# VectorE masks a dense tile inside a burst of top-k operations

## The reference, cut to what matters

```
def _pk(x, Wq_pk, pk_keys):
    q = (x @ Wq_pk).reshape(b, n, P, HEADS, DIM_KEY).transpose(2, 0, 1, 3, 4)
    sim = jnp.einsum('pbnhd,pkhd->pbnhk', q, pk_keys)
    scores, idx = jax.lax.top_k(sim, PK_TOPK)
    index = (idx0[..., :, None] + idx1[..., None, :]).reshape(b, n, HEADS, PK_TOPK * PK_TOPK)
    score = (scores[0][..., :, None] + scores[1][..., None, :]).reshape(...)
    final_scores, pk_idx = jax.lax.top_k(score, FINAL_TOPK)
    ...
k = jnp.einsum('bnhk,bnhkd->bnhd', kv_scores, keys_table[ind])
v = jnp.einsum('bnhk,bnhkd->bnhd', kv_scores, values_table[ind])
```

## Time and profile before

| what | value |
|---|---|
| median of the timed runs | 3286.44 us |
| lowest and highest | 3283.16, 3289.22 us |
| span of the profiled execution | 3919.1 us |
| TensorE busy in it | 2986.0 us (76%) |
| VectorE busy in it | 2791.8 us (71%) |
| ScalarE busy in it | 2037.7 us (52%) |
| GpSimd busy in it | 2052.1 us (52%) |
| mean granted clock of TensorE | 0.869 of full speed |

### The profile page before, as it was taken

One profiled execution on the slowest core, in us unless ns is written; L12 is line 12 of the kernel. 1 busy time (PEld: TensorE's weight loads), 2 busy tenths in 40 slices (PEclk: granted clock), 3 DMA queues, 4 the chain that ended last, 5 costly groups with the idle time before them and its releaser, 6 DMA issues. The chain is left out here.

```text
span 3919.1 us, 39389 instructions
## 1 busy us (share of the span) xinstructions
PE 2986.0 (76%) x9782; PEld 1393.2 (36%) x9782; DVE 2791.8 (71%) x9999; ACT 2037.7 (52%) x4498; POOL 2052.1 (52%) x2095
## 2 busy tenths in 40 slices
PE   4861667868786768878787878787878878787888
PEld 2430222424333323334333433333333433333443
DVE  7678777777777777777768786767768887864423
ACT  3231544555555655556555655555555755555522
POOL 3011666566666666565656655555656565655300
PEclk7985777989788989999889989888988989998999
DMA  1001121212121212111111111121211111111000
GB/s 37 22 8 52 45 66 43 59 46 58 48 58 48 58 48 59 45 53 51 54 50 48 56 45 55 41 57 44 58 45 52 53 51 48 47 56 42 23 3 3
DMA packets 85626, 179.86 MB, mean 46 GB/s; under 512 B 40177, under 2 KB 41107, under 8 KB 85398
## 3 DMA queue, kind: packets, MB, share of 16 engines
q0 software_dynamic: 66560, 135.40, 13.2%
q1 hardware_dynamic: 18838, 41.94, 3.4%
HBM read 176.15 MB, written 1.05 MB: 45 GB/s over the span
## 5 line engine op out<-in xcount | busy, mean ns | idle before, releaser
L1356 POOL DMA_INDIRECT mx_G<-in_kv_table,mx_slot_i x2048 | 1998.7, 976 | 1388.0 <-issue 605.7
L1384 PE MATMUL mx_acc<-mx_W,mx_table 128*128 128x512 f32 x2048 | 1179.6, 660 | 3.4 <-ACT mx_kvT L1586 3.2
L1743 DVE SCALAR_TENSOR_TENSOR mx_W<-mx_D,mx_W 128x512 f32<-128x512 f32 x1024 | 698.5, 682 | 352.7 <-ACT mx_W L1579 257.9
L1579 ACT ACTIVATE mx_W<-mx_D 128x512 f32<-128x512 f32 x1024 | 607.5, 594 | 525.0 <-remote 235.1
L1647 ACT ACTIVATE mx_GT<-mx_G,mx_slot_w 128x128 f32<-128x128 f32 x2048 | 759.1, 495 | 3.9 <-DVE mx_KVs L1960 1.9
L1374 PE MATMUL mx_D<-mx_U,mx_pick_b 96*128 96x512 bf16 x1024 | 434.3, 424 | 117.6 <-remote 53.8
L1384 PEld LDWEIGHTS mx_acc<-mx_W,mx_table 128*128 128x128 f32 x2048 | 437.4, 215 | 214.9 <-issue 130.4
L1603 ACT ACTIVATE mx_PT<-mx_area 128x512 f32<-128x512 f32 x480 | 246.7, 516 | 455.1 <-remote 145.2
L1396 PE MATMUL mx_O<-mx_PT,mx_KVs 128*65 128x512 f32 (+3 forms) x768 | 333.2, 517 | 130.7 <-ACT mx_OT L1595 86.7
L1410 PE MATMUL mx_area<-mx_KTa,mx_QTa 64*128 64x512 f32 (+3 forms) x384 | 202.9, 613 | 248.0 <-DVE mx_mx_part L1978 83.0
L1960 DVE TENSOR_REDUCE mx_KVs<-mx_GT 128x128 f32<-128x2048 f32 x128 | 292.0, 2281 | 7.5 <-ACT mx_GT L1647 7.3
(11 more groups left out here) (382 smaller groups left out, 4439.9 us busy)
## 6 DMA issues: line engine op xcount, KB each, us to landing
mx_table<-in_kv_dense SPq DMA_DIRECT2D x64, 512.0 KB
mx_G<-in_kv_table,mx_slot_i POOLq DMA_INDIRECT x2048
tz_table<-in_c_dft SPq DMA_DIRECT2D x1, 2048.0 KB
tz_table<-in_c_idft SPq DMA_DIRECT2D x8, 256.0 KB, 2.6
out_h<-mx_xc SPq DMA_DIRECT2D x4, 256.0 KB
mx_G<-in_c_pick SPq DMA_DIRECT2D x1, 528.0 KB
st_h<-in_tok_W,em_ids POOLq DMA_INDIRECT x32
st_keys<-in_pk_keys SPq DMA_DIRECT2D x1, 512.0 KB, 3.8
```

Of the source, the lines that this page charges most:

```text
L1356: pool.indirect_dma_start(G[g % RING][:, r, :], None, a["kv_table"], bass.IndirectOffsetOnAxis(slot_i[n % 2][:, k, r:r + 1], 0))\
L1384: pe.matmul(acc[:, :], table[:, tile, :], W[c % TILE_RING][:, :], start=(tile == 0), stop=(tile == TILES - 1)).then_inc(applied, 1)
L1579: act.activation(W[c % TILE_RING][:, :], D_ps[c % 3][:, :], ACT.Exp).then_inc(p_done, 1)
L1743: dve.scalar_tensor_tensor(W[c % TILE_RING][:, :], D_ps[c % 3][:, :], 0.0, W[c % TILE_RING][:, :], ALU.is_ge, ALU.mult).then_inc(w_done, 1)
```

## The change

In 17 of the 32 positions of the chain, the steps that are bursts now call `other_work()` too, some way into the burst: after four of eight maxima, after two of the three or four items of an index and replace step, after two of four pairs of indices in steps 9 and 10, before the third of five pairs of sums, after four of eight in steps 14, 17 and 18. The mask of the position is then done there, and not at the position's end. For 15 slots with both a top-k chain and dense tiles that is 34 masks a slot, 510 of 1024. No instruction, wait or DMA is added or taken away.

```diff
                 if k in (0, 1):
                     dve.wait_ge(x_taken, cnt.x["sim", n, 2 * tau + k] + 1)
                     for j in range(8 * k, 8 * k + 8):
+                        if j % 8 == 4:
+                            other_work()
                         done["first", k] = chain.mark(dve.max(seat(V, j, lo8), S[:, j // 4, j % 4, :]))
                 if 2 <= k < 7:
                     chain.wait(done["first", 0 if k < 4 else 1])
                     for j in range(16 * (k - 2) // 5, 16 * (k - 1) // 5):
+                        if j == 16 * (k - 2) // 5 + 2:
+                            other_work()
                         if j % 2:
...
                 if k in (7, 8):
                     chain.wait(done["struck", k - 7])
                     for j in range(8 * k - 56, 8 * k - 48):
+                        if j % 8 == 4:
+                            other_work()
...
                 if k in (9, 10):
                     chain.wait(done["second", k - 9])
                     for j in range(8 * k - 71, 8 * k - 64, 2):
+                        if j % 8 == 5:
+                            other_work()
...
                     for a0, na, nb in RECTS:
+                        if a0 == 2:
+                            other_work()
...
                 if k == 14:
                     chain.wait(done["sums"])
                     for u in range(2 * GROUP):
+                        if u == GROUP:
+                            other_work()
...
                 if k in (15, 16):
                     chain.wait(done["best", k - 15])
                     for u in range(GROUP * (k - 15), GROUP * (k - 14)):
+                        if u % GROUP == 2:
+                            other_work()
...
                 if k == 17:
                     for u in range(2 * GROUP):
+                        if u == GROUP:
+                            other_work()
...
                 if k == 18:
                     for u in range(2 * GROUP):
+                        if u == GROUP:
+                            other_work()
```

## The result

The changed kernel takes 3304.14 us (median of four, 3301.08 to 3305.12) against 3286.32 beside it (3283.16 to 3289.22): a ratio of 1.0044 on record, 95% interval 1.0032 to 1.0056. The quotient of the two medians is a little larger (1.0054, 17.8 us), with four runs on each side. A second set gave 1.0041 (1.0028 to 1.0055), and there the medians are 13.8 us apart. So the kernel is slower by some 14 us, where the forecast was +6: the sign and the main place were right, the size was not.

The account below looks back on a forecast made before the run. No engine fills the span: VectorE has more work over p = 17 to 39, TensorE over p = 40 to 63. Terms +6.0 (`add_heads`), +3 (burst waits) and -3 (masks) gave +6 us, from 3286.4 to about 3293 us, range 3283 to 3305.

Parts of the forecast that it names:

- The bound: Whole span: no engine fills it; VectorE has more work over p = 17 to 39, TensorE over p = 40 to 63.
- Rows 6: Profile rows of slot 15 at p = 5, read as layer-1 attention score products covering `add_heads`, with the chain through them.
- `add_heads` at p = 5: Slots 3 to 15: the mask passes `add_heads`, so TensorE's transposes start 0.60 us later; +6.0 us, bounds 3.6 to 7.8.
- Other things passed: `add_heads` at p = 11, 20 and 49, `combine`, layernorm, gathers and table loads: no cost, taken as 0, bounds 0 to 2.4 us.
- The wait inside the burst: VectorE stands at a late exponential with half a burst behind the mask; +3 us, bounds 0 to 8.3.
- turn from ahead to behind: Near p = 15 to 21 and 35 to 39, where VectorE stops being ahead of the exponential; there a burst wait costs 0.55 us.
- Masks that TensorE waits for: Nine of 80 waits are in changed positions and get shorter by part of a burst; -3 us, ends nothing and 7 us.
- Own criteria: Profile after: waits for `add_heads` and exponential grow, scores' waits for masks shrink, TensorE's wait for maxima changes by at most some 10 us.
- The faster rival: Earlier masks pay more: half a us saved in each of 15 slots, `add_heads` hidden, about 3279 us; chance 0.22.
- The rival of burst waits: VectorE turns from ahead to behind three times a slot, 0.5 us each in 15 slots: 22.5 us lost, 3309 us; chance 0.12.

Follow-up runs that it names:

- the second profile: The unchanged kernel profiled again, as the first profile was 632.7 us longer than its timed runs; it took 3287.9 us, with a profiled span of 3286.0.
- p = 5 alone: The kernel before with only the mask of p = 5 (step 2 of tau 0, 15 masks) moved into the divided burst, ahead of `add_heads`: 3297.1 us, ratio 1.0028.
- p = 17 to 39 alone: The kernel before with only the 165 masks of p = 17 to 22 and 35 to 39 moved into their bursts: 3292.2 us, ratio 1.0013.
- the two parts that hold these masks: Two kernels against before: only the 330 masks outside p = 5 and p = 17 to 39 moved, ratio 1.0019; only those of p = 17 to 39, 1.0013.
- without p = 5: The changed kernel with the 15 masks of p = 5 put back behind `add_heads`: 3295.4 us, ratio 1.0021 to before.
- `add_heads` first: `add_heads` put ahead of the step. At p = 5: before 0.9990, changed kernel 1.0005. At every position: before 0.9994, changed kernel 1.0002.
- divided or not: Undivided: the kernel before with the mask of p = 5 between the whole step 2 and `add_heads`, 3296.1 us, ratio 1.0027; divided: 3297.1 us, 1.0028.

## Why the prediction came out as it did

**The bound.** That the first profile was the same work with more idle time in it, and that this idle time would be gone in a timed run, held for the larger part: the second profile's span is 3286.0. That busy times would be the same did not hold, since the clock was lower in the first. And one reading took cover for slack. Rows 6 were read as layer-1 products hiding `add_heads` in slot 15. In the second profile they do, but with nothing to spare: TensorE comes to the transposes of slots 7, 11 and 15 just as `add_heads` ends, without idle time before and with 0.65 to 0.66 us after, and these stretches are 0.73 to 0.74 us longer. Only in slots 8 and 12, where p = 5 to 7 is 6.48 us before and after, are the transposes covered.

**`add_heads` at p = 5: +6.0 predicted.** Place, order and releaser were right, and the wait grew by 8.8 us (weight loads; 7.2 for products) for "some 6". The term was mis-sized: in time it is 9.2 us alone, or 7.6 taken out of the whole. The step that failed is the price of a late transpose, taken as the mask's 0.60 us and nothing else. Two things were missing. The mask also waits for its exponential with `add_heads` behind it (0.14 us in slot 7). In slots 10 and 14 this is more, since the mask of p = 4 stands in its burst too, and four maxima that were ahead of it now follow its wait. Slot 14, before:

```profile
2574.27 0.69 DVE L1743 SCALAR_TENSOR_TENSOR mx_W<-mx_D,mx_W 128x512 f32<-128x512 f32 x1 [0.80 <-ACT mx_W L1579]
...
2578.43 0.65 PE L1489 MATMUL mx_X<-mx_ident_b,mx_PC 128*96 128x128 bf16 x8 [2.15 <-DVE st_h L2007]
...
2579.13 1.02 PE L1384 MATMUL mx_acc<-mx_W,mx_table 128*128 128x512 f32 x2
```

and after:

```profile
2587.74 0.69 DVE L1743 SCALAR_TENSOR_TENSOR mx_W<-mx_D,mx_W 128x512 f32<-128x512 f32 x1 [1.30 <-ACT mx_W L1579]
...
2588.34 0.59 DVE L1759 MAX8 mx_V<-mx_S 128x8 f32<-128x64 f32 x4
...
2592.97 1.09 PE L1489 MATMUL mx_X<-mx_ident_b,mx_PC 128*96 128x128 bf16 x8 [3.22 <-DVE st_h L2025]
...
2594.28 1.92 PE L1384 MATMUL mx_acc<-mx_W,mx_table 128*128 128x512 f32 x2
```

The idle time is 3.22 - 2.15 = 1.07 us longer, and that is 0.50 from p = 4 and the rest from p = 5. Then the second thing: after the longer wait TensorE runs the same two products in 1.92 us for 1.02. The stretch is 11.58 - 7.62 = 4.0 us longer from a wait that grew by 1.07. Over the 13 slots the busy time is 4.9 us longer, and the stretches are 12.1 us longer in the trace (6.4 in that of p = 5 alone, whose time says 9.2). Not all of the 12.1 is the mask of p = 5, as slots 9, 10 and 14 show.

**Other things passed: 0 predicted (0 to 2.4).** At p = 11 TensorE does wait longer, by 0.6 us in slots 8 and 12. "TensorE has a position of its own work in between" was wrong there: the transposes of line 1498 come 0.05 us after `add_heads`. There are two such slots, 8 and 12, and not four: `add_heads` runs at p = 11 in slots 16 and 20 too, but without a step of the chain. The size is within the bounds.

**The wait inside the burst: +3 predicted (0 to 8.3).** The size of p = 17 to 39 alone, 4.3 us, is near it; the mechanism as told isn't shown. From slot 7 on no mask waits at p = 17 to 22, inside a burst or at its end, so no turn from ahead to behind costs half a burst there. That a wait inside a burst comes off later idle time, as the prediction said, is seen behind p = 48: VectorE's idle time ahead of masks, in slots 1 to 15, grows from 51.1 to 60.0 us over p = 49 to 54 and falls from 20.0 to 10.1 over p = 55 to 63. Where a wait inside a burst could be shown to cost, it was at p = 4 of slots 10 and 14, which the prediction didn't have.

**Masks that TensorE waits for: -3 predicted.** The mechanism was right and its price was not. TensorE's idle time at these waits fell by some 5 us in slots 2 to 15 (7.6 to 2.7), more than the 3 that the prediction took; 0.38 us of it in slot 3, for the 0.39 that it named for such a burst. But the two parts that hold these masks are slower by 6.2 and 4.3 us. What failed is the step from a wait to time: the prediction took each shortened wait off the sum. The runs show no gain in time, and where these 5 us are lost again stays open. The whole-span row (118.3 to 121.5) hides this, because it also has the waits for masks that didn't move, and waits put down to a mask that had ended well before. By the rule that the prediction quoted from the Trainium skill (Perfetto Trace Analysis, section Optimizing Scalar/DVE Operations), breaking up work on an engine that isn't saturated can let it complete sooner. The traces bear that out for the masks (1.80 to 1.42 us of wait in slot 3) and not for the kernel, which became slower.

**Own criteria.** The wait for `add_heads` grew, as asked, and so did VectorE's for the exponential (243.3 to 264.8). The row of scores that wait for masks didn't fall. TensorE's wait with weight loads for maxima (1978) went from 187.1 + 71.8 to 189.5 + 85.2, +15.8 us, more than the 10 that the prediction allowed. With p = 5 alone, where nothing at p = 17 to 39 moved, it is 193.3 + 88.1: so it isn't the order within that stretch. The reading behind the criterion stands: over p = 17 to 39 of slots 2 to 15 VectorE is busy for 838.9 of 855.7 us before and 841.2 of 862.5 after, 98%. The wait is a poor test of it, because it also tells how fast TensorE was: in this stretch TensorE is busy for 688.7 us and waits for maxima for 247.3 before, and 678.8 and 269.8 with p = 5 alone. Over all traces but the first the two go against each other (a correlation of -0.8). What makes the stretch itself 6.8 us longer stays open.

**The sum.** +6 + 3 - 3 became about +9, +4 and +6 by the parts' own times, which overlap, since the whole is some 14. That 3304 lies inside the forecast's bounds (3283 to 3305) is in part luck: the positions that were to give 3 us back cost 6. The faster rival had its shorter waits and not its time. The rival of burst waits named nearly this time (3309), but not for this reason: with `add_heads` ahead the bursts are divided as before, and the change costs 2 to 5 us over the same order and no longer 14. What stays open is the cost of the other positions: 0.2% without p = 5, but only 0.08 to 0.15% with `add_heads` first (1.0002 and 1.0005 over 0.9994 and 0.9990), and no single place in the traces carries it.

## What to carry to other kernels

Before an operation is put earlier in an in-order list, look at what it passes and who waits for that: the 15 masks of p = 5, of 510 moved, made half of the loss or more, because 13 of them pass `add_heads`, and 11 of these delay products for which TensorE has nothing else to do. A wait that gets shorter is not yet time: some 5 us of waits for masks went away here and the kernel got no faster by it. Price a longer wait of TensorE not by its length alone, but by the granted clock of the products behind it as well. And profile the kernel before a second time when its profiled span is far from its timed one: what seems hidden may be hidden by idle time only.

## What the runs showed of the hardware

TensorE's clock has two levels here, 2.4 and 1.2 GHz (granted 1.00 and 0.50), and it fell behind waits that were little longer. In slot 14 it was at 1.00 over the whole stretch with an idle time of 2.15 us; after 3.22 us idle two products took 1.92 us for 1.02, and a score product 0.63 for 0.38. The score products of p = 6 that took 0.63 us are 3 of 13 before, 7 and 8 in the two traces of the change, 6 with p = 5 alone, divided or not, and 1 to 5 in the others. The length of the wait doesn't settle it alone: in slots 3 to 5 of before the clock fell after 2.76 to 2.81 us, in slot 6 not after 2.81; with p = 5 alone it fell in slot 9 after 1.99 us, with an idle time of 1.53 us some 6 us earlier, and not in slot 14 after 2.74. The Trainium skill (TensorE: Matmul & The Clock Gate, section Why this matters for your kernels) names idle gaps between bursts of products as what takes the clock down in the middle of a kernel; the rows of slot 14 agree. Over the whole span the mean clock didn't fall (0.927 before, 0.929 after, TensorE busy 2801.7 and 2794.2 us). So what the clock loses at p = 6 it gains elsewhere, for the most part at places that I haven't traced (over p = 17 to 39 TensorE's busy time is 2.6 us smaller).

The first profile of before was 633 us longer than the second one of the same kernel, with 2986.0 us of TensorE's busy time for 2801.7. Waits read from it were off in both directions: 57.0 us for 27.3 at `add_heads`, but 227.9 for 258.9 at the maxima and 102.1 for 118.3 at the masks. Some products seemed to cover waits with room to spare that they only just cover.
